# Moving the weight look of stage one to the opening, and reordering the last batch's tail, in an attention and feed-forward kernel

## The chip, the cores and the metric

The kernel runs on one core of a Trainium2 chip. The metric is the device time of one execution in microseconds; all times below are microseconds from the start of the profiled span unless marked otherwise. The engines are TensorE (PE, with its weight loads PEld), VectorE (DVE), ScalarE (ACT), GpSimd (POOL) and SyncE (SP), which here issues every DMA.

## The reference

The input x is (4, 1024, 128) in float32. The result is x + LN(attention(LN(x))), followed by x + LN(ffn(LN(x))).

```python
q, k, v = heads of x @ W + b                 # 16 heads of 8
rel  = einsum('bhid,pd->bhip', q, rel_key)   # P = 256
bias = take(rel, clip(j - i + P - 1, 0, P - 1))
logits = where(j <= i, (q.k + bias) * 8**-0.5, -inf)
out = softmax(logits) @ v, joined @ Wo + bo
# ffn: silu(x@w1*s1) * (x@w2*s2); gelu(.@h1*sh1); gelu(.@h2*sh2); .@w3*s3; the w are -1, 0 or 1
```

## The kernel before

The program has three stages. **Stage one** (`sync_one`, `gpsimd_one`, `vector_one`, `scalar_one`, `tensor_one`) works through four batches of 1024 tokens. For a batch it does a layernorm, transposes by TensorE, the projections to q, k and v, and a bound on the largest score of each row (`bound`, `gap`, `shift_rest`; the row shift goes to `m_parts`). It then splits q and k into three bf16 parts each: a high part, a middle part and a low part. ScalarE writes the first two (lines 687 to 693, semaphores `s_hi` and `s_mid`), VectorE makes the remainders (573, 575) and the low parts (`low_q` line 535, `low_k` line 539, semaphore `s_low`). q is also copied in another order ("turned", `q_turned`), one copy for each part; GpSimd makes these copies in batches 0 to 2 (line 474), VectorE in batch 3 (line 634). SP stores q, k and turned q to DRAM (line 391, semaphores `s_qst`, `s_kst`, `s_rst`). ScalarE may write `q_parts` of a batch only when the turned copies of the batch before are made and its q and k stores have landed; `store` waits for both q and k of a part before it issues either.

**Stage two** (`*_two`) runs 8 units of 8 heads: scores on TensorE (line 1086), added biases on VectorE (`add`, lines 1212 and 1217), exponentials on ScalarE (line 1329), and the product with v (1111). The bias tables `even_b` and `odd_b` are filled from matmuls with `rel_w` and `q_rows` (`relative`, line 1020). For the first unit the fills of `even_b` already happen in batch 3: chunks 0 to 5 are copied by ScalarE (line 1033) and masked by GpSimd (989, 993), chunks 6 and 7 are masked by VectorE straight from PSUM (626, 627). **Stage three** is the feed-forward part.

Two flags, made at the end of stage one (lines 791, 792, 616), decide on slow paths: one says that a bound on scores is exceeded, the other that some weight of the feed-forward part has bits in its low 16 (`low_bits`, line 658, two instructions over the tile `every`, which holds all five weights; `low_max` and `low_any` are reduced from them in lines 604 and 607). Each engine reads the flags with a load (line 1455) before stage two.

The order is written out by hand: each engine has its own list of instructions and waits for semaphores, and SP's one list sets the order in which transfers are issued. In batch 1 that list is: store of the row shift of batch 0; loads of `q_rows`, `k_sb` and `q_sb` for stage two's first unit (line 408, `load_k` line 334, `load_q` line 323); the five loads of `every` (line 414); only then the nine stores of batch 1. SP's list in the opening is: x of batch 0 and 1, small weights, `bv_b`; a wait for `rel_p` and `gx` (`s_gs`); stores of these, a wait for them, the load of `g_ext`, two of `rel_w`; x of batches 2 and 3; four loads of pads and a wait until they have landed; then the stores of batch 0. `g_ext` is read by VectorE in line 555.

Of the kernel before, what the change touches and what calls it, by code (L numbers as in the profile page):

```python
# [105 lines left out]
def ap(handle, offset, dims):  # L106
    return bass.AP(handle, offset, dims)
# [47 lines left out]
def build(nc, ctx, x, Wq, bq, Wk, bk, Wv, bv, Wo, bo, rel, w1, s1, w2, s2, h1, sh1, h2, sh2, w3, s3, out):  # L155
# [191 lines left out]
    def sync_one(sp):  # L347
# [13 lines left out]
        tokens(1)  # L361
        sp.dma_start(bv_b[:, :], ap(bv.tensor, 0, [[0, 128], [1, 128]])).then_inc(s_bv, 16)

        sp.wait_ge(s_gs, 9)
# [33 lines left out]
        def batch(b, first, last):  # L398
            if b == 2:
                sp.wait_ge(s_mst, 16)  # L400
                for hg in range(2):
                    load_m(0, hg)
            if not first:
                shift(b - 1)
            if b == 1:
                for done in (s_qst, s_kst, s_rst):
                    sp.wait_ge(done, 16 * PARTS)
                sp.dma_start(q_rows[:, :], ap(qr_dram, 0, [[DROW, PARTS * HD], [0, PARTS], [1, UH * S]])).then_inc(t_qr[0], 16)
                for hg in range(2):
                    load_k(0, hg)  # L410
                    load_q(0, hg)
                c = 0
                for _, w, rows, cols in WEIGHTS:
                    sp.dma_start(every[:, c:c + rows * cols].rearrange("p (r c) -> p r c", r=rows),
                                 w.rearrange("(r p) c -> p r c", p=128)).then_inc(s_every, 16)
                    c += rows * cols
            for part, made in enumerate((s_hi, s_mid, s_low)):
                sp.wait_ge(made, b * 2 + 2)
                store(b, q_dram, (HD * DROW, DROW), part, q_parts, s_qst)
                store(b, k_dram, (DROW, PARTS * DROW), part, k_parts, s_kst)  # L420
                if not last:
                    turned(b, part)
# [60 lines left out]
    def vector_one(dve):  # L483
# [57 lines left out]
        def batch(b, first, last_batch):  # L541
# [34 lines left out]
            if not last_batch:  # L576
                biased_v(b)
                low_q(b)
                low_k(b)

        layernorm(0, True)
# [20 lines left out]
        batches(batch)  # L602
        dve.wait_ge(s_wabs, CHECKS)
        nc.vector.tensor_scalar(low_max[:, :], low_max[:, :], 0.0, None, ALU.is_gt).then_inc(s_wany, 1)
        gap(B - 1)
        dve.wait_ge(s_wany, 1)
        nc.vector.tensor_reduce(out=low_any[:, :], in_=low_max[:, :], op=ALU.max, axis=AX.X).then_inc(s_wany, 1)
        dve.wait_ge(s_gap, B)
# [8 lines left out]
                                axis=AX.X).then_inc(s_gap, 1)  # L617
        low_k(B - 1)
        dve.wait_ge(s_last, 4)
# [9 lines left out]
        dve.wait_ge(s_last, 4 + FILL - FIRST_ACT)  # L629
        dve.wait_ge(s_rst, 16 * PARTS * (B - 1))  # L630
        for part in range(PARTS):
            if part == 2:
                dve.wait_ge(s_low, B * 2 - 1)
            nc.vector.tensor_copy(turned_view(q_turned, part), untouched_view(q_parts, part)).then_inc(s_turned, 1)
        dve.wait_ge(s_gap, B + 3)
        dve.wait_ge(s_low, B * 2)

    def scalar_one(act):
# [22 lines left out]
        def batch(b, first, last_batch):  # L661
# [9 lines left out]
            if first:  # L671
                root(1)
            if b == 2:
                low_bits(0)
            if not last_batch:
# [18 lines left out]

            if b == 2:
                low_bits(1)
            if not first:
# [5 lines left out]
            if last_batch:  # L703
                for c in range(FIRST_BEFORE, FIRST_ACT):
                    copy_act(act, "even", c)
                nc.scalar.activation(exp_warm[:, :], ident[:, 0:1], ACT.Exp, scale=0.0)

        root(0)
# [1337 lines left out]
```

## Time and profile before

| what | us |
|---|---|
| median of 3 runs | 748.63 |
| lowest and highest run | 745.51, 749.91 |
| profiled execution, its own time | 748.76 |
| its span | 747.0 |
| busy TensorE / VectorE / ScalarE / GpSimd | 638.3 / 555.4 / 550.7 / 269.3 |
| mean DMA rate | 71 GB/s |

The span is what the profile sees; the execution's own time is 1.76 longer. Stage one lasts to about 121 to 125, stage two to about 536, stage three to the end. In stage two and three TensorE is busy nine tenths of nearly every slice; the slices in which it is not lie in the first 125 us.

### The profile page before, as it was taken

The page shows a single profiled execution, that of the slowest core. Times are in us where ns is not written, and L with a number is a line of the kernel's source. Part 1 is how long each engine was busy: PE and PEld are TensorE (multiplying, and loading weights), DVE is VectorE, ACT ScalarE, POOL GpSimd, SP SyncE. Part 2 cuts the span into 40 slices and gives each one's busy share as a digit, 9 for nine tenths or more (in the row PEclk, how much of TensorE's full clock was granted, in tenths as well). Part 3 has the DMA queues.
Part 4 walks back from the last instruction along what each step waited for, and adds up shares of the span by engine and source line. Part 5 has one row for each costly group of instructions (what it writes and reads, how often), then busy time and mean ns, then how long its engine had stood idle before and what let it go on. Part 6 is the DMA issues. An engine that isn't in the chain of part 4 may idle for free.

```text
span 747.0 us, 18943 instructions
## 1 busy us (share of the span) xinstructions
PE 638.3 (85%) x8066; PEld 463.8 (62%) x8066; DVE 555.4 (74%) x926; ACT 550.7 (74%) x648; POOL 269.3 (36%) x184
## 2 busy tenths in 40 slices
PE   4862766999999999999999999986799899998993
PEld 2431324676676676766766767655588687786682
DVE  5896699778678788787786877777577668578546
ACT  2441763888988989889889898887577868677572
POOL 2331471073190450721805508101181451730901
PEclk9986775999999999999999999998899999999997
DMA  2669622223142142231421422241200000000001
GB/s 76 174 153 269 225 70 81 67 68 97 34 99 72 45 115 65 67 98 33 104 80 42 114 56 67 67 127 45 82 18 2 0 1 0 1 29 0 6 24 59
DMA packets 39177, 52.85 MB, mean 71 GB/s; under 512 B 5656, under 2 KB 29640, under 8 KB 36680
## 3 DMA queue, kind: packets, MB, share of 16 engines
q1 hardware_dynamic: 39088, 51.58, 25.5%
q8 instruction: 66, 1.08, 0.6%
q14 instruction: 23, 0.19, 0.1%
HBM read 39.00 MB, written 11.81 MB: 68 GB/s over the span
## 4 chain that ended last, share of the span: by engine, by line
PE 50%; DVE 13%; ACT 12%; issue 5%; POOL 2%; DVEq 0%; ACTq 0%; POOLq 0%
PE p_o L1111 15%; PE p_s L1086 12%; PE p_z L1785 8%; PE p_z L1788 8%; DVE probs L1212 7%; ACT probs L1329 6%; PE p_s L1020 4%; POOL hid_lo L1706 1%; DVE res L1966 1%; ACT hid_hi L1889 1%; ACT o_acc L1338 1%; ACT even_b L1033 1%; ACT odd_b L1033 1%; PE p_o L1123 1%; DVE hid_lo L1990 1%
## 5 line engine op out<-in xcount | busy, mean ns | idle before, releaser
L1086 PE MATMUL p_s<-q_sb,k_sb 96*128 96x128 bf16 (+1 forms) x1600 | 169.5, 247 | 12.2 <-DVE probs L1212 3.1
L1329 ACT ACTIVATE probs<-p_s 128x1024 f32<-128x1024 f32 x160 | 156.8, 1018 | 24.3 <-DVE p_s L1221 10.9
L1111 PE MATMUL p_o<-probs,v_sb 128*32 128x128 f32 (+1 forms) x3200 | 156.6, 327 | 7.7 <-ACT o_acc L1338 4.6
L1329 ACT ACTIVATE probs<-probs 128x1024 f32<-128x1024 f32 x128 | 133.5, 1055 | 34.0 <-DVE probs L1212 33.9
L1086 PEld LDWEIGHTS p_s<-q_sb,k_sb 96*128 96x128 bf16 x1600 | 111.1, 99 | 70.7 <-issue 29.7
L989 POOL TENSOR_SCALAR_AFFINE_SELECT even_b<-even_b 128x2048 f32<-128x2048 f32 x31 | 74.1, 2391 | 215.9 <-ACT even_b L1033 215.9
L1212 DVE TENSOR_TENSOR probs<-p_s,even_b 128x1024 f32<-128x1024 f32 x96 | 114.9, 1218 | 15.7 <-PE p_s L1086 15.6
L1111 PEld LDWEIGHTS p_o<-probs,v_sb 128*32 128x32 f32 x3200 | 83.8, 110 | 39.9 <-issue 12.0
L1785 PE MATMUL p_z<-hid_hi,h_hi 128*128 128x512 f32 x256 | 102.2, 399 | 1.8 <-POOL hid_lo L1706 1.8
L1788 PE MATMUL p_z<-hid_lo,h_hi 128*128 128x512 f32 x256 | 100.8, 394 | 0.0
L1020 PE MATMUL p_s<-q_rows,rel_w 72*128 72x64 bf16 x2048 | 83.1, 195 | 15.8 <-DVE probs L1212 8.7
L1020 PEld LDWEIGHTS p_s<-q_rows,rel_w 72*128 72x128 bf16 x2048 | 74.7, 100 | 27.2 <-DVE probs L1212 10.6
L1990 DVE TENSOR_TENSOR hid_lo<-act_f,hid_hi 128x512 fp32r<-128x512 f32 x64 | 54.9, 870 | 42.1 <-ACT hid_hi L1889 42.0
L993 POOL TENSOR_SCALAR_AFFINE_SELECT even_b<-even_b 128x2048 f32<-128x2048 f32 x31 | 75.4, 2432 | 7.3 <-POOL even_b L989 7.3
L1888 ACT ACTIVATE act_f<-p_z,sh_c 128x512 f32<-128x512 f32 x64 | 44.4, 694 | 28.6 <-PE p_z L1788 28.5
L1233 DVE COPY even_b<-p_s 128x1024 f32<-128x1024 f32 x35 | 42.7, 1220 | 21.2 <-PE p_s L1020 21.0
L1785 PEld LDWEIGHTS p_z<-hid_hi,h_hi 128*128 128x128 f32 x256 | 48.2, 188 | 13.8 <-POOL hid_lo L1706 2.6
L1788 PEld LDWEIGHTS p_z<-hid_lo,h_hi 128*128 128x128 f32 x256 | 48.2, 188 | 10.7
L1233 DVE COPY odd_b<-p_s 128x896 f32<-128x896 f32 x32 | 34.7, 1086 | 22.6 <-PE p_s L1020 22.6
L1212 DVE TENSOR_TENSOR probs<-p_s,odd_b 128x1024 f32<-128x1024 f32 x32 | 39.1, 1222 | 13.0 <-PE p_s L1086 13.0
L474 POOL COPY q_turned<-q_parts 128x1024 bf16<-128x1024 bf16 x9 | 24.8, 2766 | 59.0 <-ACT q_parts L687 53.3
L1889 ACT ACTIVATE hid_hi<-p_z,sh_c 128x512 fp32r<-128x512 f32 x64 | 44.1, 690 | 0.0
(183 smaller groups left out, 880.8 us busy)
## 6 DMA issues: line engine op xcount, KB each, us to landing
k_sb<-k_dram SPq DMA_DIRECT2D x48, 192.0 KB
q_sb<-q_dram SPq DMA_DIRECT2D x16, 576.0 KB
q_rows<-qr_dram SPq DMA_DIRECT2D x42, 192.0 KB
q_dram<-q_parts SPq DMA_DIRECT2D x12, 256.0 KB, 3.0
k_dram<-k_parts SPq DMA_DIRECT2D x12, 256.0 KB, 3.2
qr_dram<-q_turned SPq DMA_DIRECT2D x12, 256.0 KB, 3.1
x_all<-in_L_attn_x_dram SPq DMA_DIRECT2D x4, 512.0 KB, 4.3
every<-in_L_ffn_h_w_dram SPq DMA_DIRECT2D x2, 1024.0 KB, 16.0
```

Of the source, the lines that this page charges most:

```text
L989: nc.gpsimd.affine_select(out=far, in_=near, compare_op=ALU.is_ge, fill=0.0, base=-1 - r, pattern=[[0, QB], [-1, MCH * RCH]], channel_mult ...
L993: nc.gpsimd.affine_select(out=near, in_=near, compare_op=ALU.is_ge, fill=MASKED, base=r, pattern=[[0, QB], [1, MCH * RCH]], channel_multip ...
L1020: last = nc.tensor.matmul(slot[:, x * QB:(x + 1) * QB], rel_w[0:ROWS, w0:w0 + BLK], q[:, r, :, :], start=True, stop=True)
L1086: last = nc.tensor.matmul(slot[:, c:c + n * BLK], k_sb[hg][:, h * S + j * BLK:h * S + (j + 1) * BLK], ap(q_sb[hg], at, [[HG * S, KROWS], [ ...
L1111: last = nc.tensor.matmul(p_o[32 * h:32 * h + 32, at:at + blocks * BLK], v_sb[hg][:, j, h * 32:(h + 1) * 32], probs[n % PBUFS][:, h, col * ...
L1212: last = nc.vector.tensor_tensor(probs[m % PBUFS][:, hp * 2:hp * 2 + 2, :], columns(slot, 0, run), term, ALU.add)
L1233: nc.vector.tensor_copy(to, got).then_inc(t_cd, 1)
L1329: nc.scalar.activation(to, got, ACT.Exp, scale=SCALE).then_inc(t_exp, 1)
L1785: nc.tensor.matmul(to[:, :], whi[w][:, j, cols], hi[j], start=(j == 0), stop=False)
L1788: last = nc.tensor.matmul(to[:, :], whi[w][:, j, cols], lo[j], start=False, stop=(j == len(hi) - 1))
L1889: nc.scalar.activation(hid_hi[k][l % 2][:, o, :], bank(tile)[:, :], ACT.Gelu, scale=sc).then_inc(f_ghi, 1)
L1990: nc.vector.tensor_tensor(hid_lo[k][l % 2][:, o, :], act_f[k][:, o, :], hid_hi[k][l % 2][:, o, :].bitcast(F32), ALU.subtract).then_inc(f_l ...
```

## The change

There are four edits. The five loads of `every` move in SP's list from batch 1 to the opening, directly behind `bv_b`. The two looks at it (`low_bits`) move on ScalarE from batch 2 to batches 0 and 1 (to where the first stood, behind `kf`). The two small VectorE operations on the result (`low_max`, `low_any`) move from behind batch 3 to the end of batch 2. At the end of stage one, VectorE's `low_k` of batch 3 moves behind the masks of chunks 6 and 7, and the three turned copies of batch 3 move from the end of VectorE's list to the end of ScalarE's batch 3, behind the warm-up of the exponential.

```diff
@@ sync_one
         sp.dma_start(bv_b[:, :], ...).then_inc(s_bv, 16)
+        c = 0
+        for _, w, rows, cols in WEIGHTS:
+            sp.dma_start(every[:, c:c + rows * cols].rearrange("p (r c) -> p r c", r=rows),
+                         w.rearrange("(r p) c -> p r c", p=128)).then_inc(s_every, 16)
+            c += rows * cols
         sp.wait_ge(s_gs, 9)
...
                     load_q(0, hg)
-                c = 0
-                for _, w, rows, cols in WEIGHTS:
-                    sp.dma_start(every[...], w...).then_inc(s_every, 16)
-                    c += rows * cols
@@ vector_one, end of batch(b)
                 low_k(b)
+            if b == CHECKS:
+                dve.wait_ge(s_wabs, CHECKS)
+                nc.vector.tensor_scalar(low_max[:, :], low_max[:, :], 0.0, None, ALU.is_gt).then_inc(s_wany, 1)
+                dve.wait_ge(s_wany, 1)
+                nc.vector.tensor_reduce(out=low_any[:, :], in_=low_max[:, :], op=ALU.max, axis=AX.X).then_inc(s_wany, 1)
@@ vector_one, behind batch 3
-        dve.wait_ge(s_wabs, CHECKS)
-        nc.vector.tensor_scalar(low_max[:, :], ...)
         gap(B - 1)
-        dve.wait_ge(s_wany, 1)
-        nc.vector.tensor_reduce(out=low_any[:, :], ...)
...
-        low_k(B - 1)
         dve.wait_ge(s_last, 4)
         for c in range(FIRST_ACT, FILL):
             ...
         dve.wait_ge(s_last, 4 + FILL - FIRST_ACT)
-        dve.wait_ge(s_rst, 16 * PARTS * (B - 1))
-        for part in range(PARTS):
-            if part == 2:
-                dve.wait_ge(s_low, B * 2 - 1)
-            nc.vector.tensor_copy(turned_view(q_turned, part), untouched_view(q_parts, part)).then_inc(s_turned, 1)
+        low_k(B - 1)
@@ scalar_one, batch
-            if b == 2:
-                low_bits(0)
+            if b < CHECKS:
+                low_bits(b)
...
-            if b == 2:
-                low_bits(1)
...
                 nc.scalar.activation(exp_warm[:, :], ident[:, 0:1], ACT.Exp, scale=0.0)
+                act.wait_ge(s_rst, 16 * PARTS * b)
+                for part in range(PARTS):
+                    act.wait_ge((s_hi, s_mid, s_low)[part], b * 2 + 1)
+                    nc.scalar.activation(turned_view(q_turned, part), untouched_view(q_parts, part),
+                                         ACT.Identity).then_inc(s_turned, 1)
```

## Rows read from the trace of the kernel before

**Rows 1.** Table by stretch: length, busy per engine, granted clock, DMA share, GB/s.
```profile
44.00:67.00 23.00, 16.19 (x52) 8.47 (x52) 22.09 (x46) 9.54 (x12) 9.53 (x5) 0.80 0.79 174
67.00:81.00 14.00, 2.25 (x3) 1.18 (x4) 1.53 (x3) 5.20 (x6) 0.00 (x0) 0.50 0.97 354
```
**Rows 2.** Timeline of ScalarE and VectorE, batches 2 and 3: start, duration, engine, line, operation.
```profile
75.09 2.55 ACT L658 ACTIVATE low_part<-every 128x2816 f32<-128x2816 uint16 x1 [13.70 <-DMA every<-in_L_ffn_w_w_dram]
...
80.36 1.06 ACT L687 ACTIVATE q_parts<-qf 128x1024 bf16<-128x1024 f32 x1 [0.71 <-DMA k_dram<-k_parts]
...
88.43 1.21 DVE L539 TENSOR_TENSOR k_parts<-k_rest,k_parts 128x1024 bf16<-128x1024 f32 x1
...
92.77 1.22 DVE L550 TENSOR_REDUCE k_ext<-kf 128x1 f32<-128x1024 f32 x1 [0.15 <-ACT kf L670]
```
**Rows 3.** Timeline of SP's DMA issues.
```profile
14.95 0.55 SPq L368 DMA_DIRECT2D g_ext<-gx_dram  x1
...
31.24 0.63 SPq L391 DMA_DIRECT2D q_dram<-q_parts  x1
...
44.28 0.83 SPq L408 DMA_DIRECT2D q_rows<-qr_dram  x1
...
51.55 11.90 SPq L414 DMA_DIRECT2D every<-in_L_ffn_h_w_dram  x2
...
72.45 1.17 SPq L391 DMA_DIRECT2D k_dram<-k_parts  x1
```
**Rows 4.** DMA issues by line: count, KB each, median us to landing.
```profile
every<-in_L_ffn_h_w_dram SPq DMA_DIRECT2D x2, 1024.0 KB, 16.0
...
every<-in_L_ffn_w_w_dram SPq DMA_DIRECT2D x3, 256.0 KB, 18.6
...
bv_b<-in_L_attn_bv_dram SPq DMA_DIRECT2D x1, 64.0 KB, 4.0
```
**Rows 5.** DMA packets, stretch 67 to 68.
```profile
DMA packets 433, 0.27 MB, mean 269 GB/s; under 512 B 16, under 2 KB 397, under 8 KB 433
```
**Rows 6.** DMA packets, stretch 68 to 75.
```profile
DMA packets 1734, 2.83 MB, mean 404 GB/s; under 512 B 87, under 2 KB 440, under 8 KB 1734
```
**Rows 7.** Timeline of ScalarE and VectorE, batches 0 and 1.
```profile
24.43 1.09 ACT L648 ACTIVATE xT<-p_tr 128x512 f32<-128x512 f32 x2 [3.52 <-PE p_tr L728]
...
25.89 0.16 DVE L555 TENSOR_TENSOR k_ext<-k_ext,g_ext 128x2 f32<-128x2 f32 x1
...
45.09 0.60 ACT L648 ACTIVATE xT<-p_tr 128x512 f32<-128x512 f32 x1 [4.18 <-PE p_tr L728]
...
47.33 1.05 ACT L687 ACTIVATE q_parts<-qf 128x1024 bf16<-128x1024 f32 x1
```
**Rows 8.** Timeline of all engines, the end of stage one.
```profile
105.79 2.32 DVE L604 TENSOR_SCALAR low_max<-low_max 128x2 f32<-128x2 f32 x1
...
106.05 1.02 PE L758 MATMUL p_tr<-own,hneg 128*64 128x512 f32 x2
...
113.19 0.41 DVE L616 TENSOR_REDUCE flags<-p_tr 1x2 int32<-1x256 f32 x1
113.53 3.02 DVE L539 TENSOR_TENSOR k_parts<-k_rest,k_parts 128x1024 bf16<-128x1024 f32 x1
...
115.03 1.01 PE L1086 MATMUL p_s<-q_sb,k_sb 96*128 96x256 bf16 x4 [0.94 <-issue]
116.47 1.21 DVE L626 TENSOR_TENSOR even_b<-p_s,far_keep 128x1024 f32<-128x1024 f32 x1
...
116.58 1.02 ACT L1329 ACTIVATE probs<-p_s 128x1024 f32<-128x1024 f32 x1 [5.34 <-DVE k_parts L539]
...
121.11 2.95 DVE L634 COPY q_turned<-q_parts 128x1024 bf16<-128x1024 bf16 x3
...
123.98 1.08 DVE L1233 COPY odd_b<-p_s 128x896 f32<-128x896 f32 x1
124.98 3.56 DVE L1212 TENSOR_TENSOR probs<-p_s,even_b 128x1024 f32<-128x1024 f32 x3
```

More of the change, by code:

```diff
@@ L411, in batch @@
                     load_q(0, hg)
-                c = 0
-                for _, w, rows, cols in WEIGHTS:
-                    sp.dma_start(every[:, c:c + rows * cols].rearrange("p (r c) -> p r c", r=rows),
-                                 w.rearrange("(r p) c -> p r c", p=128)).then_inc(s_every, 16)
-                    c += rows * cols
             for part, made in enumerate((s_hi, s_mid, s_low)):
@@ L602, in vector_one @@
         batches(batch)
-        dve.wait_ge(s_wabs, CHECKS)
-        nc.vector.tensor_scalar(low_max[:, :], low_max[:, :], 0.0, None, ALU.is_gt).then_inc(s_wany, 1)
         gap(B - 1)
-        dve.wait_ge(s_wany, 1)
-        nc.vector.tensor_reduce(out=low_any[:, :], in_=low_max[:, :], op=ALU.max, axis=AX.X).then_inc(s_wany, 1)
         dve.wait_ge(s_gap, B)
```

## The prediction

> **What bounds the kernel now.** I read the page's 40 slices first. TensorE is nearly full from 125 us to the end, so the change, which touches only stage one and the seam to stage two, can win or lose only in the first 125 us. I then asked for stretches of that part, and after them for SP's timeline and that of ScalarE and VectorE. From 67 to 81 TensorE is busy for 2.25 of 14 us and VectorE for 1.53, while the DMA engines are busy for 0.97 of the time at 354 GB/s [rows 1]. That is one hole in the program. ScalarE stands for 13.70 us in front of the first look until the last part of `every` lands at 75.09; it then makes xT and q_pos, and stands once more until 80.36 for a store of k of batch 1 [rows 2]. The second wait matters more: even without the first, ScalarE couldn't write `q_parts` before 80.36. The reader should see why that store is so late. SP starts the loads of q_rows at 44.28 and k_sb and q_sb behind it, then turns to `every`: its two h loads occupy the issuing engine from 51.55 for 11.90 us and the last one for more, and the last k store of batch 1 is issued only at 72.45 [rows 3]. So `every` delays those stores twice, in SP's list and in the DMA rings. Outside this hole VectorE bounds stage one: 22.09 of 23 us busy from 44 to 67 [rows 1].
>
> I call T the moment at which ScalarE starts `q_parts` of batch 2 (80.36 now) and price the change as a move of T and moves behind T.
>
> **Part 1, the loads leave batch 1.** The five loads are 2 x 1024 + 3 x 256 KB [rows 4], 2.88 MB. When they and the stores ran, the rings moved 404 GB/s [rows 6], which makes 7.1 us. The rings were never empty between 44.28 and 80.3, and what stays (the loads for stage two, 3.5 MB, and nine stores of 256 KB) has to go through before the k stores have landed. SP is then ready for the stores as each part is made, and all nine are issued by about 59. So T = 80.36 - 7.1 = 73.2. A cross-check: the packets from 67 to 68 are all under 8 KB [rows 5], so the q and k loads (rows of 8 KB) had ended at 67. Nine stores of 256 KB behind them at 404 GB/s take 5.8 us: 72.8. The lower bound for T is 67.8, where ScalarE would come to this instruction with no wait (`kf` of batch 2 ends 61.4, xT needs transposes that end 66.3, q_pos 67.8). The upper bound is 80.36, which holds if the quarter of DMA time unused from 44 to 67 (share 0.79, [rows 1]) shows that the rate there is set by something that `every` didn't slow. I take 73.2, the nearest to both counts.
>
> The Trainium skill, "DMA: Bandwidth & Descriptors", section "Why a DMA increments its semaphore by 16 and not by 1", says that a DMA runs on the largest number of engines up to 16 that divides the slowest dimension of both sides. These loads have 24 rows at the source, so 12 engines, and four stay free; the share of 0.79 agrees. By that rule the nine stores end where the 12 loaded engines end, which is the 72.8 of the cross-check, and not earlier.
>
> **Part 2, the loads enter the opening.** SP has issued `bv_b` by 6.3 and then waits for `s_gs` until 13.4, so five issues (some 0.6 each) are hidden unless the rings push back. `bv_b`, issued at 5.7, lands 4.0 later [rows 4]; from 9.7 the rings have only `every`. At 404 GB/s it is in by 17, with about a us to land: L = 18. At the rate of 44 to 67, 174 GB/s [rows 1], L would be 26.5. I take 18, since these are rows of 512 and 2048 bytes like those of rows 6. The stores of rel_p and gx, issued at 13.4, now stand behind `every` in the rings. They had landed when `g_ext` was issued, at 14.95 [rows 3], and will at L + 1 = 19; `g_ext` needs 2.8 us more, 22 to 22.4, and VectorE reads it at 25.89 [rows 7]: hidden by 3.5 us. All of SP's list behind it (rel_w, x of batches 2 and 3, pads, and the wait for the pads) shifts by 4: the first store of batch 0 goes at 35.3 instead of 31.24 [rows 3]. By then nearly all parts are made (the last turned one at 37.95), so nine issues of 0.64 end at 41.1, and the data (2.36 MB at 300 to 400 GB/s) has landed at 42 to 44. It has to be in for the q_rows load at 44.28 [rows 3] and for `q_parts` of batch 1 at 47.33 [rows 7]. So the shift costs 0, with little cover left for the loads: each us of L beyond 18.5 is a us of T. With L = 26.5 it is 8.5.
>
> The look in batch 0 is 2.55 + 0.19, and falls into an idle stretch of 3.52 on ScalarE before xT at 24.43; that in batch 1 into one of 4.18 before 45.09 [rows 7]. Both are free (worst, if `every` lands after 21.7: the lateness, up to L + 2.7 - 24.4).
>
> **Part 3, batch 2 behind T.** ScalarE loses the second look (2.7), but VectorE bounds here: it works from q_rest (T + 1.1) to k_ext of batch 3 at 92.77, T + 12.4 [rows 2], with some 0.7 of waits inside. These go; 0.4 is added by `low_max` and `low_any` (0.17 and 0.16 uncontended, and a wait). Gain 0.3.
>
> **Part 4, batch 3.** `low_max` took 2.32 us there [rows 8], over two elements, beside a GpSimd mask; it ended at 108.11, and only then `gap` started, while the last matmul of `bound` had ended at 107.07 [rows 8]. Gain 1.0, and 0.2 for `low_any`. GpSimd's masks begin about 3 us earlier against VectorE, and may hold k_sel or k_rest longer: -0.5 (between 0 and -3, one mask). Together with part 3: 1.0.
>
> **Part 5, the seam.** The flags end at 113.60. Now low_k follows (3.02), then four masks from 116.47 to 121.1 (4.6), then three turned copies to 124.06, and the first copy of odd_b at 123.98 [rows 8]. After: four masks 4.6, low_k 1.2 (GpSimd's last mask ends at 115.5, and the same pass took 1.21 in batch 2 [rows 2]), and then a wait for low_k and the load of the flags, no longer hidden behind queued copies; TensorE took 1.4 from the flags' end to its first scores at 115.03 [rows 8]. Sum 7.2, so odd_b at 120.9 on the old scale: gain 3.1. The added wait: ScalarE's first exponential waits for all of low_k, so it moves from 116.58 [rows 8] to 119.5. TensorE's third scores need its slot: 120.6 + 1.0 = 121.6, and VectorE's first add would start at 122.0 (124.98 now). So this wait is just hidden; what comes late next is this chain, 0.4 behind. The last q and k stores are issued 3 us later too (119.6 and 120.2, landed by 123.5), before the fifth step asks for them at about 124.2. ScalarE's turned copies cost at most 3 x 1.05: two from 111.2, the last behind low_q at 113.3, all done by 114.4, in its idle 5.34 [rows 8].
>
> The Trainium skill, "SBUF — State Buffer", section "Who interferes with whom", says that a VectorE instruction with two SBUF inputs is kept waiting by a GpSimd instruction that reads SBUF, and one with a PSUM input isn't. The trace agrees: low_k takes 3.02 beside a mask and 1.21 alone. By it the masks moved forward keep their 1.2; with 3.02 for low_k instead the gain of part 5 would be 1.3.
>
> **Sum.** 7.1 + 1.0 + 3.1 = 11.2. From 748.76, the profiled execution's time, 737.6. That execution lies 0.13 over the median of 748.63, so I forecast 737.5 for the median. In stage two nothing else shifts, since all engines start it later or earlier together.
>
> **The rivals.**
> - *The stores stop binding* (T near 67.8): gain 12.6 + 4.1, 732. For it: the unused DMA time. Against it: the 67.0 at which the loads end. 0.10.
> - *The opening costs some*: L of 21 to 23, T + 3 to 4.5: gain 7 to 8, 741. For it: small rows and three other loads in flight. 0.15.
> - *Part 1 doesn't do what it says*: the stores land at about 80 anyway, gain 4.1, 744.7. Against it: 404 GB/s from 68 to 75, a full ring. 0.07.
> - *Slower, the opening jams.* `every` took from 49.76 to 75.09 to land; if it takes these 25.3 us from 6.3, L = 31.6. Then `g_ext` is read 9 us late, the stores of batch 0 start at 31.24 + 17, and T = L + 55.2 (73.2 - 18) = 86.8, a loss of 6.4 against gains of 4.1: 751. The point from which it decides is L = 29.3; beyond 32.8 it is slower by over 0.5%. For it: SP was held for 11.90 us by one pair [rows 3]. Against it: the rings held 3.5 MB of slow loads then, and only 0.5 MB of x now. 0.05.
> - The forecast itself, 734 to 740: 0.63.
>
> 0.5% (3.7 us) is about what a measurement of this kernel tells from no change; the three runs differ by 4.4. Faster by more: 0.63 + 0.10 + 0.15 and about half of the 744.7 case, 0.91. Within: 0.06. Slower: 0.03. The range of eight in ten, with the cases at 732 and 741 mostly inside: 731.5 to 742.5.
>
> **What would show it.** `every` lands by 18 to 20; the first q store goes at 35; q_rows still at 44 to 45; `q_parts` of batch 2 starts at 73 (71 to 75); ScalarE has no wait of more than 1 us for `every`; low_k is last on VectorE in stage one, 1.2 long; the first add on even_b comes at 113 to 115 instead of 124.98. The prediction is wrong if q_rows goes after 46, if T is above 77, or if stage two, measured from that first add to the end, isn't of the same length within 1 us.

## The result, and the profile after

The median of 20 runs of the changed kernel is 743.44 us (740.61 to 746.69) against 748.69 for 20 runs of the kernel before on the same chips: a ratio of 0.9931 with an interval of 0.9915 to 0.9947, a gain of 5.2. It was measured twice more beside other kernels: 0.9913 (0.9884 to 0.9942) and 0.9922 (0.9907 to 0.9937), gains of 6.5 and 5.8. The forecast was a gain of 11.2. So the change makes the kernel faster, by about half of what I said, and 743.4 lies outside the range of 731.5 to 742.5.

The slice table by stretch first (columns as in [rows 1]).

```profile
44.00:67.00 23.00, 17.28 (x50) 7.90 (x49) 22.09 (x47) 11.56 (x15) 9.48 (x5) 0.80 0.79 192
67.00:81.00 14.00, 12.23 (x35) 5.11 (x33) 8.18 (x6) 6.61 (x8) 6.54 (x3) 0.85 0.59 197
```

The stretch from 44 to 67 is as full as before. From 67 to 81 TensorE works for 12.23 us where it had 2.25, and the DMA engines, at 0.97 before, stand at 0.59: the hole of [rows 1] is mostly closed. Now the DMA issues on SP's timeline, which answer to [rows 3].

```profile
7.34 1.68 SPq L365 DMA_DIRECT2D every<-in_L_ffn_h_w_dram  x2
...
18.61 0.55 SPq L373 DMA_DIRECT2D g_ext<-gx_dram  x1
...
34.64 0.63 SPq L396 DMA_DIRECT2D q_dram<-q_parts  x1
...
44.20 0.84 SPq L413 DMA_DIRECT2D q_rows<-qr_dram  x1
...
56.45 2.65 SPq L396 DMA_DIRECT2D k_dram<-k_parts  x1
59.15 3.55 SPq L396 DMA_DIRECT2D qr_dram<-q_turned  x1
```

The opening went as forecast: `g_ext` is issued at 18.61 (19 was forecast), the first store of batch 0 at 34.64 (35.3), and `q_rows` still at 44.20. The stores of batch 1 are out by 62.7 instead of 72.45 and later. Their tail is 3.7 us behind my 59, because SP is held in two issues of 2.65 and 3.55 us while the q and k loads fill the rings; in `loads_late` below, which issues these loads later, the same two took 0.60 and 0.52. On ScalarE's timeline:

```profile
19.77 2.54 ACT L654 ACTIVATE low_part<-every 128x2816 f32<-128x2816 uint16 x1
...
23.39 1.09 ACT L644 ACTIVATE xT<-p_tr 128x512 f32<-128x512 f32 x2 [0.99 <-PE p_tr L727]
...
39.75 2.55 ACT L654 ACTIVATE low_part<-every 128x2816 f32<-128x2816 uint16 x1
...
72.19 1.06 ACT L683 ACTIVATE q_parts<-qf 128x1024 bf16<-128x1024 f32 x1 [6.13 <-DMA k_dram<-k_parts]
...
97.80 1.06 ACT L687 ACTIVATE q_parts<-q_rest 128x1024 bf16<-128x1024 f32 x1 [9.78 <-DVE q_rest L573]
...
106.40 5.85 ACT L704 ACTIVATE q_turned<-q_parts 128x1024 bf16<-128x1024 bf16 x3
...
113.39 1.94 ACT L1328 ACTIVATE probs<-p_s 128x1024 f32<-128x1024 f32 x2 [1.14 <-DVE k_parts L539]
```

Both looks are free: there is no wait in front of either, and xT of batch 0 even starts a us before that in [rows 7]. T, ScalarE's `q_parts` of batch 2, comes at 72.19 instead of 80.36. What stands in front of it is still the landing of the k stores, for 6.13 us. The row at 97.80 is what to look at next: ScalarE stands 9.78 us in batch 3 for VectorE. VectorE's timeline there, from `low_max` in batch 2 to the first add on `even_b`, which answers to [rows 8]:

```profile
81.39 1.91 DVE L582 TENSOR_SCALAR low_max<-low_max 128x2 f32<-128x2 f32 x1
...
88.27 1.11 DVE L555 TENSOR_TENSOR k_ext<-k_ext,g_ext 128x2 f32<-128x2 f32 x1
89.42 2.27 DVE L558 TENSOR_TENSOR k_ext<-k_ext 128x1 f32<-128x1 f32 x1
91.73 2.60 DVE L563 TENSOR_SCALAR k_sel<-hmask,k_ext 128x64 f32<-128x64 f32 x2
94.23 1.27 DVE L567 SCALAR_TENSOR_TENSOR own<-kf,g_ext,qf 128x1024 f32<-128x1024 f32 x1
...
96.56 1.21 DVE L573 TENSOR_TENSOR q_rest<-qf,q_parts 128x1024 f32<-128x1024 f32 x1
97.69 1.21 DVE L575 TENSOR_TENSOR k_rest<-kf,k_parts 128x1024 f32<-128x1024 f32 x1
...
102.47 1.22 DVE L515 TENSOR_REDUCE gap_max<-p_tr 16x1 f32<-16x1024 f32 x1 [3.57 <-PE p_tr L757]
...
106.45 0.41 DVE L617 TENSOR_REDUCE flags<-p_tr 1x2 int32<-1x256 f32 x1
...
112.14 1.22 DVE L539 TENSOR_TENSOR k_parts<-k_rest,k_parts 128x1024 bf16<-128x1024 f32 x1
...
115.62 1.23 DVE L1211 TENSOR_TENSOR probs<-p_s,even_b 128x1024 f32<-128x1024 f32 x1
```

From 88.27 on four instructions (k_sel is two, in one row) over 2, 1 and 64 elements take 5.98 us in sum. GpSimd's timeline over the same time shows why (L988 and L992 are the masks):

```profile
80.39 2.88 POOL L474 COPY q_turned<-q_parts 128x1024 bf16<-128x1024 bf16 x1 [1.15 <-DVE q_parts L535]
84.44 2.36 POOL L988 TENSOR_SCALAR_AFFINE_SELECT even_b<-even_b 128x2048 f32<-128x2048 f32 x1 [1.17 <-ACT even_b L1032]
87.03 2.36 POOL L992 TENSOR_SCALAR_AFFINE_SELECT even_b<-even_b 128x2048 f32<-128x2048 f32 x1 [0.23 <-POOL even_b L988]
89.34 2.36 POOL L988 TENSOR_SCALAR_AFFINE_SELECT even_b<-even_b 128x2048 f32<-128x2048 f32 x1
91.92 2.36 POOL L992 TENSOR_SCALAR_AFFINE_SELECT even_b<-even_b 128x2048 f32<-128x2048 f32 x1 [0.23 <-POOL even_b L988]
```

Each of the slow ones ends as a mask does: 89.38 beside 89.39, 91.69 beside 91.70, 94.33 beside 94.28. `low_max` ends at 83.30, with the turned copy that ends at 83.27. Two of the masks' neighbours, the reduces for `k_ext` at 85.91 and 87.04, are not held (1.20 each). In the kernel before GpSimd's first mask starts 15.4 us behind T, here 12.2. GpSimd's timeline and VectorE's in the kernel before:

```profile
95.73 2.36 POOL L989 TENSOR_SCALAR_AFFINE_SELECT even_b<-even_b 128x2048 f32<-128x2048 f32 x1 [4.27 <-ACT even_b L1033]
```

```profile
95.15 0.16 DVE L555 TENSOR_TENSOR k_ext<-k_ext,g_ext 128x2 f32<-128x2 f32 x1
95.35 0.16 DVE L558 TENSOR_TENSOR k_ext<-k_ext 128x1 f32<-128x1 f32 x1
95.54 2.59 DVE L563 TENSOR_SCALAR k_sel<-hmask,k_ext 128x64 f32<-128x64 f32 x2
...
100.37 2.22 DVE L573 TENSOR_TENSOR q_rest<-qf,q_parts 128x1024 f32<-128x1024 f32 x1
102.51 3.35 DVE L575 TENSOR_TENSOR k_rest<-kf,k_parts 128x1024 f32<-128x1024 f32 x1
```

Both `k_ext` instructions had passed before the first mask began, and only one mask was waited for: 2.9 us in all against 6.0. The masks of the kernel before held other instructions instead: the remainders `q_rest` and `k_rest` took 2.22 and 3.35 there, and take 1.21 each here, where the first four masks are over by 94.28. But the remainders run while TensorE works on `bound` (99.45 to 107.07 there), so most of that hold cost nothing. The change moved the meeting from instructions with slack to a chain that `bound` waits for.

Where the time is, from three profiles of each kernel (means, with the three values in brackets; each value is a start or a difference of starts in those traces, and `own` is the instruction at 94.23, behind which `bound` starts):

| stretch | before | after | gain | forecast |
|---|---|---|---|---|
| start to T | 79.23 (80.36, 78.92, 78.42) | 72.87 (72.19, 73.58, 72.84) | 6.4 | 7.1 |
| T to flags | 32.65 (32.83, 32.34, 32.77) | 34.74 (34.26, 35.41, 34.54) | -2.1 | 1.0 |
| T to own, part of the row above | 17.8 (17.68, 18.07, 17.62) | 22.0 (22.04, 22.03, 22.03) | -4.2 | |
| flags to first add | 11.75 (11.79, 11.68, 11.77) | 8.85 (9.17, 8.45, 8.92) | 2.9 | 3.1 |
| first add to the end of the span | 623.4 (622.0, 626.2, 622.0) | 624.3 (624.7, 623.1, 625.3) | -0.9 | 0 |

Part of the last row is no scatter. In the kernel before, three first blocks of scores are ready for VectorE when it comes (the row of x3 at 124.98 in [rows 8]); in the changed kernel it starts on the first alone and then waits for TensorE. So the first add comes earlier than the rest of the unit does. Up to VectorE's first reciprocal into `o_rcp`, near the end of the first unit (166.02 before, 157.10 after in the first pair), the time from the flags is 52.8, 53.3 and 52.8 before and 50.7 in all three traces after. By that mark the seam gives 2.3, and 0.6 of the last row's 0.9 goes with it.

### The profile page after: what moved, and what is told of

Read it like the earlier page. It is cut to its first block, busy times and chain, and to the rows that moved or that the text cites. A ratio compares the mean times of both kernels' runs of the same rounds, so it can differ in the third digit from the quotient of the medians.

```text
span 740.3 us, 18944 instructions
## 1 busy us (share of the span) xinstructions
PE 641.5 (87%) x8066; PEld 465.0 (63%) x8066; DVE 550.6 (74%) x923; ACT 556.3 (75%) x651; POOL 266.9 (36%) x184
## 3 DMA queue, kind: packets, MB, share of 16 engines
q8 instruction: 65, 1.06, 0.6%
## 4 chain that ended last, share of the span: by engine, by line
PE 52%; DVE 13%; ACT 12%; issue 5%; POOL 2%; DVEq 0%; ACTq 0%; POOLq 0%
PE p_o L1110 16%; PE p_s L1085 12%; PE p_z L1784 8%; PE p_z L1787 8%; DVE probs L1211 6%; ACT probs L1328 6%; PE p_s L1019 5%; POOL hid_lo L1705 1%; DVE res L1965 1%; ACT hid_hi L1888 1%; ACT o_acc L1337 1%; ACT even_b L1032 1%; ACT odd_b L1032 1%; PE p_o L1122 1%; DVE hid_lo L1989 1%
## 5 line engine op out<-in xcount | busy, mean ns | idle before, releaser
L1110 PE MATMUL p_o<-probs,v_sb 128*32 128x128 f32 (+1 forms) x3200 | 159.2, 330 | 7.5 <-ACT o_acc L1337 4.7
L1085 PEld LDWEIGHTS p_s<-q_sb,k_sb 96*128 96x128 bf16 x1600 | 112.7, 100 | 67.8 <-issue 30.4
L988 POOL TENSOR_SCALAR_AFFINE_SELECT even_b<-even_b 128x2048 f32<-128x2048 f32 x31 | 74.3, 2396 | 219.8 <-ACT even_b L1032 219.8
L1211 DVE TENSOR_TENSOR probs<-p_s,even_b 128x1024 f32<-128x1024 f32 x96 | 114.9, 1218 | 16.5 <-PE p_s L1085 16.4
L992 POOL TENSOR_SCALAR_AFFINE_SELECT even_b<-even_b 128x2048 f32<-128x2048 f32 x31 | 73.1, 2358 | 7.3 <-POOL even_b L988 7.3
L1232 DVE COPY odd_b<-p_s 128x896 f32<-128x896 f32 x32 | 34.7, 1086 | 23.7 <-PE p_s L1019 22.5
L1211 DVE TENSOR_TENSOR probs<-p_s,odd_b 128x1024 f32<-128x1024 f32 x32 | 39.1, 1222 | 13.8 <-PE p_s L1085 13.8
L1705 POOL TENSOR_TENSOR hid_lo<-act_f,hid_hi 128x512 fp32r<-128x512 f32 x32 | 42.4, 1325 | 2.6
```

Of the source, the lines that this page charges most:

```text
L988: nc.gpsimd.affine_select(out=far, in_=near, compare_op=ALU.is_ge, fill=0.0, base=-1 - r, pattern=[[0, QB], [-1, MCH * RCH]], channel_mult ...
L992: nc.gpsimd.affine_select(out=near, in_=near, compare_op=ALU.is_ge, fill=MASKED, base=r, pattern=[[0, QB], [1, MCH * RCH]], channel_multip ...
L1085: last = nc.tensor.matmul(slot[:, c:c + n * BLK], k_sb[hg][:, h * S + j * BLK:h * S + (j + 1) * BLK], ap(q_sb[hg], at, [[HG * S, KROWS], [ ...
L1110: last = nc.tensor.matmul(p_o[32 * h:32 * h + 32, at:at + blocks * BLK], v_sb[hg][:, j, h * 32:(h + 1) * 32], probs[n % PBUFS][:, h, col * ...
L1211: last = nc.vector.tensor_tensor(probs[m % PBUFS][:, hp * 2:hp * 2 + 2, :], columns(slot, 0, run), term, ALU.add)
L1232: nc.vector.tensor_copy(to, got).then_inc(t_cd, 1)
```

## The experiments

All kernels start from the changed one unless it is said otherwise. Ratios are to the kernel before on the same chip. The two kernels run again (the kernel before gave 0.9996, 0.9984 to 1.0008, and 1.0001, 0.9983 to 1.002) supply the table above. Their expectations:

> The changed kernel as it is, once more, for a second trace and a second ratio. First theory: the 2.7 us that its profile lost between the first add and the end against the kernel before are stretches at half clock that fall by chance; then the first add comes again at 115 to 117, the median ratio is 0.993 plus or minus 0.002, and the stretches at half clock in stage two lie elsewhere and differ in number. Second theory: stage two of the changed kernel is slower for a reason of its own; then the same two units (around 370 and 420 us) are again 1.2 to 1.4 us longer than 49.3. Third: the first profile caught a lucky stage one; then the first add comes at 117 or later.

> The kernel before, once more, for a second trace. Its first trace is the only one with a single short stretch at half clock at the end of stage two and none inside the units; from its first add to the end it took 622.05 us, against 623.05 to 626.0 in the five others. If that was chance, it takes 623 to 626 this time and the span is 748 to 751. If stage two of the kernel before is really shorter, it takes 622 again, and the later start of stage two is part of the reason.

> The kernel before a third time: first add at 123 to 125, span 747 to 750, from the first add to the end 622 to 626.5 as in all fourteen traces. A first add outside 122 to 126 would mean that the difference of the two pairs of traces is itself mostly chance.

> The changed kernel a third time. Its first add came at 115.62 and 117.44, the kernel before's at 124.98 and 122.94: 7.4 earlier on the mean, of which 0.3 goes into the time outside the span; the two ratios so far say 5.2 (4.0 to 6.4) and 6.5 (4.3 to 8.7). If the whole gain of the seam reaches the end, the third ratio is 0.990 to 0.992 (6 to 7.5 us) and the first add is at 115 to 118; if part of it is lost in stage two, 0.993 to 0.994 with the same first add.

**The halves alone.** `loads_only` has the seam of before (low_k ahead of the masks, turned copies on VectorE); `seam_only` is the kernel before with the new seam.

```diff
 # loads_only, vector_one (and the turned copies leave scalar_one)
 # seam_only = before, with these the other way round
+        low_k(B - 1)
         dve.wait_ge(s_last, 4)
...
         dve.wait_ge(s_last, 4 + FILL - FIRST_ACT)
-        low_k(B - 1)
+        for part in range(PARTS): ... tensor_copy(turned_view(...))
```

> The changed kernel with the seam of before: loads and looks moved, but low_k ahead of the masks and the turned copies of batch 3 on VectorE. If the parts add up as the two traces show them (8.2 gained up to T, 1.4 lost from T to the flags, 2.6 gained at the seam), its first add comes at 118.2 and it is 2.6 us slower than the changed kernel, 2.7 faster than before. If the loads bring nothing on the whole time it equals the kernel before.

> The kernel before with the new seam alone: masks of chunks 6 and 7 first, then low_k, turned copies of batch 3 on ScalarE; loads and looks as before. By the traces the seam brings 2.6 to 3.1: first add at 122 instead of 124.98 and 746. If low_max beside the GpSimd mask costs what the prediction said, gap still starts at 108. If the seam gains nothing because the exponentials wait for low_k, the first add stays at 124 to 125.

`loads_only`: 745.37, 0.9937 (0.9913 to 0.9961), T at 72.98. `seam_only`: 748.60, 0.9988 (0.9972 to 1.0005), T at 79.51. From T to the flags the first takes 34.97 and the second 33.27: the loss behind T comes with the moved loads and looks. From VectorE's timeline, first `loads_only` (its `k_ext` and k_sel are as slow as in the changed kernel), then `seam_only`:

```profile
89.07 1.09 DVE L555 TENSOR_TENSOR k_ext<-k_ext,g_ext 128x2 f32<-128x2 f32 x1
...
108.28 1.20 DVE L539 TENSOR_TENSOR k_parts<-k_rest,k_parts 128x1024 bf16<-128x1024 f32 x1
...
117.99 3.56 DVE L1211 TENSOR_TENSOR probs<-p_s,even_b 128x1024 f32<-128x1024 f32 x3
```
```profile
112.78 0.41 DVE L616 TENSOR_REDUCE flags<-p_tr 1x2 int32<-1x256 f32 x1
...
121.23 1.23 DVE L1212 TENSOR_TENSOR probs<-p_s,even_b 128x1024 f32<-128x1024 f32 x1
```

The old seam behind the moved loads takes 117.99 - 107.95 = 10.04, not the 11.75 of before: low_k, 3.02 beside a mask in [rows 8], is already 1.20 here, since the masks are done. So the two halves aren't additive: 1.7 of the seam's 2.9 come with the loads, and 1.2 remain for the reordering. Up to the reciprocal (51.3 from the flags in `loads_only`) 0.6 remain; the ratio of `loads_only`, 0.9937, is 0.5 to 1.8 us above the three of the changed kernel, within the noise. In `seam_only` the seam (121.23 - 112.78) takes 8.45, 3.3 less than in the kernel before, and the first add comes 2.4 earlier than its mean there; of that the ratio shows 0.9, and its interval reaches to 2.1. Alone, this half can't be told from no change.

**The masks and VectorE's small instructions.** `masks_wait` holds GpSimd's masks until both remainders of batch 3 are made; `masks_split` holds only the second and third pair of chunks; `max_back` puts `low_max` and `low_any` back behind batch 3; `both` is `masks_split` and `max_back` together.

```diff
 # gpsimd_one
+        pool.wait_ge(s_rest, B * 2)              # masks_wait
         for m in range(FIRST_ACT // MCH):
+            if m == 1:                           # masks_split
+                pool.wait_ge(s_rest, B * 2)
             masks(pool, 0, m)
```

> The changed kernel, with GpSimd's masks of chunks 0 to 5 held until k_rest of batch 3 is made. In the changed kernel six tiny VectorE operations (lines 555, 558, 563) take 6.0 us beside these masks, against 0.74 in batch 2, and bound of batch 3 starts 5 us late. If that costs the path, own of batch 3 comes at 89 instead of 94.2, the flags 3 to 5 us earlier, and the kernel is 3 to 4 us faster than the changed one. If the masks themselves become late (they would end at 111 to 112), the first add waits for them and the gain is 0 to 2. If batch 3 is bound by something else, nothing changes.

> The changed kernel, with only the masks of chunks 2 to 5 held until k_rest of batch 3; those of chunks 0 and 1 run at once. Holding all gained 4.9 us at the flags but only 3.1 at the first add, because low_k then ran beside a mask again (3.29). Here own should come some 1.1 later than with all held (one small operation waits for the second select), and low_k alone (1.2), so the first add 1 us earlier than with all held. If low_k stays at 3 us the split brings nothing.

> The changed kernel, with the two small operations on low_max back behind batch 3, where they stood before. In the changed kernel they take 2.1 us in VectorE's busy stretch (1.91 of them for two elements, beside a turned copy on GpSimd), while VectorE now idles 3.6 to 4.8 us ahead of the last gap. If that stretch is the path, gap of batch 2, own of batch 3 and the first add all come 2.1 us earlier relative to the first q_parts of batch 2, and the kernel gains 1 to 2 us. If GpSimd's masks only hold the next operations longer (they are the bound through their lock on the small operations), own gains less than 1.

> The two edits together, as a candidate for the best version. If both costs are separate, the first add comes at 110 to 112 (T at 73) and the kernel is 4 to 5 us faster than the changed one, 738. If the lock of GpSimd's first two selects takes what low_max gives back, it equals the better of the two.

| kernel | us | ratio | T | T to own | T to flags | T to first add |
|---|---|---|---|---|---|---|
| changed (mean of three) | 743.0 to 744.1 | 0.9913 to 0.9931 | 72.87 | 22.0 | 34.7 | 43.6 |
| masks_wait | 741.08 | 0.9884 (0.9857 to 0.991) | 73.06 | 16.8 | 29.8 | 40.3 |
| masks_split | 737.87 | 0.9848 (0.9823 to 0.9874) | 73.45 | 17.8 | 30.0 | 39.2 |
| max_back | 740.26 | 0.988 (0.9847 to 0.9912) | 73.11 | 19.5 | 33.2 | 41.7 |
| both | 739.36 | 0.9843 (0.9827 to 0.986) | 71.80 | 17.3 | 30.9 | 39.4 |

VectorE's timeline in `masks_split`, then in `max_back`:

```profile
89.52 1.14 DVE L557 TENSOR_TENSOR k_ext<-k_ext,g_ext 128x2 f32<-128x2 f32 x1
90.69 0.16 DVE L560 TENSOR_TENSOR k_ext<-k_ext 128x1 f32<-128x1 f32 x1
90.89 0.42 DVE L565 TENSOR_SCALAR k_sel<-hmask,k_ext 128x64 f32<-128x64 f32 x2
```
```profile
87.94 4.72 DVE L563 TENSOR_SCALAR k_sel<-hmask,k_ext 128x64 f32<-128x64 f32 x2
...
98.17 0.15 DVE L604 TENSOR_SCALAR low_max<-low_max 128x2 f32<-128x2 f32 x1
```

With the masks away `k_ext` and k_sel cost 0.16 and 0.42 again (the first of them, 1.14, still waits for the pair of masks that is not held), and the way from T to the flags is 4.7 to 4.9 shorter, with nothing else changed than when the masks start. That shows the cause of 4.3 to 5.2 us between T and own; all of these kernels have one trace each. `masks_wait` pays for it later: the masks now run beside low_k (3.29 us at 107.83), which `masks_split` avoids by letting one pair go early (low_k 1.23). `max_back` gains 1.5 to the flags, and `low_max` costs 0.15 in its place there. But it runs k_sel into two masks in a row (4.72), so that `both` isn't better than `masks_split` alone.

**TensorE's clock.** A rival for the loss behind T: `bound` of batch 3 runs at the lower of TensorE's two levels, 1.2 GHz, for three to seven of its twelve matmuls (0.85 us each instead of 0.43). `warm` puts six extra matmuls (twelve passes, results unused) ahead of it.

```diff
 # tensor_one, last batch, ahead of bound(b)
+                ...                          # three waits
+                for _ in range(6):
+                    nc.tensor.matmul(p_tr[:, 0:512], ident[:, :], qf[:, 0:512], start=True, stop=True)
```

> The changed kernel, with six extra matmuls (identity times qf, into p_tr, whose result is overwritten) on TensorE between the fills of chunks 0 to 3 and bound of batch 3. bound starts there after 10 us of idle TensorE and runs its first three to seven matmuls at half clock (0.85 instead of 0.43 each): 6.7 to 8 us instead of 5.3. If the clock is what makes it long, it now takes 5.3 to 6 and the flags come 1 to 2 us earlier. If the extra matmuls come too early and the clock falls again, nothing changes; if they run into own's end, bound starts later.

On TensorE's timeline:

```profile
86.40 7.08 PE L774 MATMUL p_tr<-qf,ident 128*128 128x512 f32 x12 [1.16 <-DVE m_parts L521]
...
95.89 1.04 PE L756 MATMUL p_tr<-q_pos,k_sel 128*64 128x512 f32 x2 [2.40 <-DVE own L568]
96.77 1.82 PE L757 MATMUL p_tr<-qf,k_sel 128*64 128x512 f32 x2
```

742.32, 0.9909 (0.9877 to 0.994). The extra work ended 2.4 us ahead of the bound. The first pair ran at the full clock (1.04, where the changed kernel has 1.94), the next two at the lower level (1.82 and 1.91), and the bound took 7.0 us (6.8, 8.0 and 7.2 in the three traces of the changed kernel); T to the first add is 42.9. So this edit hardly moved the clock, and it says nothing on what a higher one would give. In the kernel before the first pair took 1.94 as well and the bound 7.6 to 7.8. The clock costs both kernels something and doesn't explain the loss between T and own, which lies ahead of the bound.

What a higher clock gives stands in `late_split_warm` below, where the extra matmuls ran until the bound began (89.71). TensorE's timeline there:

```profile
89.63 1.07 PE L758 MATMUL p_tr<-q_pos,k_sel 128*64 128x512 f32 x2
```

All twelve matmuls of the bound ran at the full clock, and it took 5.4 us against 7.8 in `late_split`. But the extra work had held TensorE, so that the bound began 2.35 later (89.63 against 87.28) and ended at 95.0, where it had ended at 95.1. Extra matmuls that end where `own` does weren't run.

**What still holds T.** The row at 72.19 waits for k stores that stand in the rings behind the loads of `k_sb` and `q_sb`. `loads_late` issues those behind the stores of batch 1.

```diff
 # sync_one
             if b == 2:                    # behind the nine stores of batch 1
+                for hg in range(2):
+                    load_k(0, hg)
+                    load_q(0, hg)
...
-                for hg in range(2):       # in batch 1, behind q_rows
-                    load_k(0, hg)
-                    load_q(0, hg)
```

> The changed kernel, with the loads of k_sb and q_sb for stage two issued behind the nine stores of batch 1 instead of ahead of them (q_rows stays ahead). In the changed kernel ScalarE still idles 6.1 to 6.5 us for a k store of batch 1. If that is the time of these loads in the rings (two halves of 6.6 us each), the stores land by 65 and the first q_parts of batch 2 comes at 66 to 67 instead of 72 to 73.6, as soon as q_pos is done, and the kernel gains 5 to 6 us. If the stores themselves or q_rows are the limit, it comes at 70 or later. If the loads then hold batch 2's stores, the wait returns at q_parts of batch 3 and the gain is smaller.

> Loads behind the stores and the masks of chunks 2 to 5 held until k_rest of batch 3: the candidate. If the two costs are separate, 5 to 6 us below the split alone, that is 0.977 to 0.98 of the kernel before (732 to 734). If the earlier batch 2 only waits elsewhere, it equals the split alone.

> The candidate with the six extra matmuls ahead of bound of batch 3. If TensorE's half clock lengthens bound there too, 1 to 2 us less than without them; if not, equal or up to 2 us more.

> As loads_late, but the store of the row shift of batch 1 is issued ahead of the k_sb and q_sb loads instead of behind them. In loads_late ScalarE idled 5.36 us in batch 2 for that store (it sat behind 2.3 MB in the rings). If that is the path, m_parts of batch 2 comes at 73 to 74 instead of 77.8, and the first add 3 to 4 us earlier, 103 to 104 (731 to 732). If batch 2's q and k stores are then late behind the loads, the wait only moves to q_parts of batch 3, and it equals loads_late (735).

> The same with the masks of chunks 2 to 5 held until k_rest of batch 3. With T at 66 and no wait in batch 2 it starts batch 3 as the split kernel did after its T (first add at T + 39.2): 105 to 106 if VectorE's order allows no more, 103 if the hold of the small operations was still there in the other.

ScalarE's and VectorE's timelines in `loads_late`:

```profile
65.84 1.06 ACT L683 ACTIVATE q_parts<-qf 128x1024 bf16<-128x1024 f32 x1
...
77.79 1.06 ACT L695 ACTIVATE m_parts<-p_tr 16x512 bf16<-16x512 f32 x2 [5.36 <-DMA m_dram<-m_parts]
```
```profile
83.26 0.16 DVE L555 TENSOR_TENSOR k_ext<-k_ext,g_ext 128x2 f32<-128x2 f32 x1
...
83.65 0.42 DVE L563 TENSOR_SCALAR k_sel<-hmask,k_ext 128x64 f32<-128x64 f32 x2
...
106.67 1.23 DVE L1211 TENSOR_TENSOR probs<-p_s,even_b 128x1024 f32<-128x1024 f32 x1
```

The wait at T is gone altogether, T comes 7 us earlier, and the time is 735.06, 0.9816 (0.9789 to 0.9843): 13.8 below the kernel before by the ratio, and with the four kernels built on it the lowest that ran. The row shift of batch 1, now stored behind the loads, became the next wait (5.36), and with that delay ScalarE's copies of `even_b` come later: the first mask starts at 84.12, just behind the end of k_sel. Holding the masks adds nothing to that: `late_split` 735.49, 0.9822 (0.9794 to 0.985); with the extra matmuls 735.71, 0.9821 (0.9793 to 0.9848). `late_shift` puts that store ahead of the loads: its wait goes (2.16 on TensorE's bound instead), but k_sel takes 2.52 again and the first add stays at 106.57; 736.11, 0.9821 (0.9799 to 0.9844). `late_shift_split`: 736.43, 0.9818 (0.9802 to 0.9835). These five can't be told apart. All have first adds of 106.6 to 108.6. So the hopes of 731 to 734 in the expectations weren't met, and `late_shift` equals `loads_late`, as its other branch said. The first add comes 40.1 to 40.9 behind T in all five, against 39.2 in `masks_split`. In the four built on `loads_late` the first mask starts 16.5 to 16.9 behind T, and k_sel waits for it again (2.5 to 2.6). What else holds the first add wasn't settled.

## Why the prediction was wrong, step by step

- **Part 1** (T 80.36 to 73.2, 7.1): right in mechanism and nearly in size, 6.4 over three pairs. The kernel before has its T at 78.4 to 80.4, and I had read the latest of them; the forecast of the new T, 73.2, is within its 72.2 to 73.6. Luck helped the size: the 7.1 stand on 404 GB/s, and in the changed kernel the rings moved 271 to 309 GB/s from 66 to 72, when the last stores landed; in exchange they moved more before (192 against 174 GB/s from 44 to 67). The share of 0.79 in that stretch is a mean; from 54 to 60, before the stores were issued, it was 0.74 to 0.75 in the kernel before, which is nearer to the 12 of 16 engines of the forecast. `loads_late` shows what the rest of the hold is, the q and k loads. With T at 65.84, and at 66.1 to 67.7 in the four kernels built on it, it also shows that my lower bound of 67.8 was none.
- **Part 2** (the opening costs nothing): right, with `every` landed before the first look asked for it.
- **Parts 3 and 4** ("GpSimd's masks begin about 3 us earlier against VectorE, and may hold k_sel or k_rest longer: -0.5 (between 0 and -3, one mask). Together with part 3: 1.0"): this is the step that failed: the range of one mask for what a meeting with GpSimd can cost, and the 0.4 for `low_max` and `low_any`. Measured: -2.1 where 1.0 was forecast. The masks did come 3 us earlier (12.2 behind T instead of 15.4), because ScalarE no longer made the second look ahead of its copies of `even_b`. I priced one longer instruction. What happens is a dependent chain of which three instructions are held, each until the mask then running ends: 5.98 us instead of 2.91, so 3.1 lost, more than my -3 bound. `low_max` and `low_any`, priced at 0.4, took 2.1 beside a turned copy on GpSimd. I had used 2.32 for the same instruction beside a mask as a gain in part 4 and its uncontended 0.17 as the cost in part 3, without asking what GpSimd does at its new place. So 5.2 were lost. 3.1 came back. 0.9 are waits that went between T and own. 2.1 lie between own and the flags: 1.0 because `gap` now starts as soon as `bound` ends, and 0.2 for `low_any`, both as part 4 had them; 0.7 because `low_q`, ahead of the flags, took 2.19 beside a mask in two of the three traces of before and takes 1.20 now, which I had not priced; and 0.3 because `bound` happened to be shorter (7.3 on the mean against 7.7). This gives the -2.1. `masks_split` shows the first loss: with the masks held, 30.0 from T to the flags, 1.6 less than parts 3 and 4 forecast (32.65 - 1.0). The second is seen in `max_back`, where `low_max` costs 0.15 ahead of a wait for `bound`; the flags gained 1.5 of its 2.1 there.
- **Part 5** (the seam, 3.1): right in mechanism, 2.9 at the first add, but only 2.3 at the end of the first unit; that the first add would run ahead of TensorE's next scores was not in the sum. The credit is shared: the masks that hurt in batch 3 are gone by low_k, as `loads_only` shows with 1.7 of it. The added wait of the first exponential is there (1.14 at 113.39) and hidden.
- **"In stage two nothing else shifts"**: not quite. In all 18 traces the length from the first add to the end was 622.0 to 626.2, whatever the kernel; my test of 1 us was finer than the kernel repeats. Sum at the first add: 123.63 - 116.45 = 7.2. Of this 0.6 goes in the first unit (above), 0.3 in the scatter of stage two, and 0.3 outside the span, which leaves 6.0; the ratios say 5.2 to 6.5. The part outside the span is 1.7 to 1.8 in the kernels with the old seam, `loads_only` too, and 2.1 to 2.2 in all with the new one, `seam_only` too (time of the profiled execution less its span). What that 0.3 is wasn't settled.
- A figure of the rivals: the opening that jams costs over 0.5% beyond L = 33.0 by its own numbers (29.3 + 3.7), not 32.8. Nothing rests on it.

Two rivals came nearer to 743.4 than the forecast did, "part 1 doesn't do what it says" with 744.7 and "the opening costs some" with 741, both for reasons that didn't occur. No rival was about VectorE and GpSimd, though the price of one such meeting, 2.32 us for two elements, stood in [rows 8].

The Trainium skill, "SBUF — State Buffer", section "Who interferes with whom", names VectorE instructions with two SBUF inputs as those that wait for GpSimd, and reduces as free of it. The traces agree for the reduces (k_ext at 85.91 and 87.04 took 1.20 each beside masks, as anywhere) and for the two tensor_tensor ones. The same section lists tensor_scalar among the operations that can take the ports shared with GpSimd; `low_max` and k_sel, a tensor_scalar each, waited too (1.91, and up to 4.72 for k_sel's two).

## What to carry to other kernels

Before an instruction is moved, look at what the other engine does at its new place; the price of a tiny VectorE instruction of the kinds held here (tensor_tensor and tensor_scalar; the reduces weren't) is then not its own 0.16 us but the rest of the GpSimd instruction beside it, once for each such link of a dependent chain. Ask too whether the instruction has slack: the same masks cost little while they met the remainders, which ran beside `bound`. When work is taken off an engine (ScalarE's second look), ask what it now starts earlier (its copies, and with them the masks), and hold that back with a wait if it collides: that was worth 4.4 us here by the traces (39.2 against 43.6 from T to the first add), 5.5 by the ratios (0.9848 against 0.9922). And when a wait goes to a transfer, ask what else stands ahead of it in the same rings: the loads needed last had been issued first.

## What the runs showed of the hardware

- Turned copies (a strided read of bf16) take ScalarE 1.95 us each, 5.85 for three; VectorE made the three in 2.95 [rows 8], and ScalarE's contiguous pass over as many elements takes 1.06. I had priced 1.05. The idle stretch hid it.
- Twelve extra passes of matmul that ended 2.4 us ahead of the bound gave only its first pair the full clock (1.04, then 1.82 and 1.91, in `warm`); with no pause between, all twelve matmuls had it (`late_split_warm`, 5.4 us in all against 7.8).
- GpSimd's masks were lengthened in their turn: one took 2.36 us as a rule, and 3.21 and 3.32 in the kernel before where VectorE made the remainders beside it (masks from 98.32 and 101.48).
- The same pause of TensorE in stage two is followed by the full clock in one unit and by less in the next. The table by stretch of the changed kernel, columns as before:

```profile
316.70:318.70 2.00, 0.76 (x18) 0.48 (x17) 2.00 (x3) 1.15 (x2) 0.00 (x0) 1.00 0.05 12
318.70:322.70 4.00, 4.00 (x70) 2.44 (x67) 3.04 (x5) 3.79 (x5) 0.00 (x0) 1.00 0.35 102
...
366.00:368.00 2.00, 0.76 (x18) 0.48 (x17) 2.00 (x3) 1.14 (x2) 0.00 (x0) 1.00 0.15 37
368.00:372.00 4.00, 4.00 (x45) 2.49 (x45) 2.47 (x4) 2.67 (x4) 0.00 (x0) 0.57 0.31 87
```

Behind 318.70 the granted clock stays at 1.00 and 70 matmuls pass in 4 us; behind 368 it is 0.57, that is mostly the lower level, and only 45 pass. That unit took 50.8 us where 49.31 is usual. The first profiles of before and after had none and two such units, those of the second pair two and none, those of the third none and two. This is most of the scatter of 622.0 to 626.2. That it isn't an effect of the change isn't shown by so few; but four traces with the moved loads and the new seam in them (`after_again`, `warm`, `max_back`, `late_shift_split`) had no such unit either.
